# One strided tensor_reduce for unit (1,2), and the first half's sums restored in 32x32 tiles

## What is computed

```python
# block 1
g = groupnorm(x)                                   # 32 groups of 4 channels
q, k, v = einsum('bchw,oc->bohw', g, w_qkv)        # each cut into 4 units of 32 channels
for i, dil in enumerate((1, 2, 4, 8)):             # unit i: 2 heads of 16 channels
    attn = softmax(q . k over the 3x3 neighbours at distance dil)   # 9 scores per pixel
    outs[i] = sum over the 9 neighbours of attn * v                 # neighbours outside the image are 0
x = x + concat(outs[i] * gate[i])                  # gate: softmax over 4 of pooled g
# block 2
p = W_qkv @ groupnorm(x) + b_qkv                   # q = k = v = p, 4 heads of 32 channels
att = softmax(p p^T * scale)                       # 32 x 32 per head
x = x + W_proj @ (att @ p) + b_proj
```

## Time and profile before

| | us |
|---|---|
| median of 3 runs | 83.01 (82.57 to 83.01) |
| the profiled execution | 83.13 |
| its span in the trace | 81.3 |

### The profile page before, as it was taken

One profiled execution on the slowest core, in us unless ns is written; L12 is line 12 of the kernel. 1 busy time (PEld: TensorE's weight loads), 2 busy tenths in 40 slices (PEclk: granted clock), 3 DMA queues, 4 the chain that ended last, 5 costly groups with the idle time before them and its releaser, 6 DMA issues.

```text
span 81.3 us, 2474 instructions
## 1 busy us (share of the span) xinstructions
PE 71.1 (87%) x1010; PEld 51.4 (63%) x1010; DVE 67.5 (83%) x184; ACT 29.3 (36%) x92; POOL 41.5 (51%) x84
## 2 busy tenths in 40 slices
PE   4999998799995698999969797879999999999950
PEld 4999753466742466776857664567676868575530
DVE  2152999999999989999999699889999888597850
ACT  1762765963384000000030003230994271764200
POOL 7104018912930037999999999699990005100000
PEclk9999999999999999999999999999999999999999
DMA  1980055000000000000000000000000000012253
GB/s 27 315 286 18 0 120 142 7 0 8 0 0 4 0 12 0 0 0 4 8 0 0 0 0 0 8 0 0 0 0 8 0 0 12 0 57 72 73 194 129
DMA packets 2796, 3.06 MB, mean 38 GB/s; under 512 B 352, under 2 KB 2400, under 8 KB 2784
## 3 DMA queue, kind: packets, MB, share of 16 engines
q1 hardware_dynamic: 2496, 2.63, 10.5%
q10 hardware_dynamic: 288, 0.26, 0.9%
HBM read 1.84 MB, written 1.05 MB: 36 GB/s over the span
## 4 chain that ended last, share of the span: by engine, by line
DVE 54%; PE 28%; POOL 7%; issue 5%; ACT 2%; POOLq 0%
PE ps L815 27%; DVE qk L602 18%; DVE pv L643 12%; POOL rstd L342 3%; POOL acc L379 3%; DVE acc L655 3%; DVE pv L655 2%; DVE x L674 2%; DVE prob L622 2%; DVE smax L609 2%; DVE ssum L619 2%; POOL pv L379 2%; DVE sums L570 1%; DVE acc L643 1%; PE ps L972 1%
## 5 line engine op out<-in xcount | busy, mean ns | idle before, releaser
L815 PE MATMUL ps<-prob,sel 64*128 64x192 f32 (+6 forms) x192 | 17.8, 313 | 2.7 <-DVE pv L643 1.6
L643 DVE TENSOR_TENSOR pv<-ps,v 128x128 f32<-128x128 f32 (+7 forms) x32 | 17.1, 567 | 1.8 <-PE ps L815 0.8
L815 PEld LDWEIGHTS ps<-prob,sel 64*128 64x128 f32 x192 | 13.7, 186 | 6.9 <-DVE pv L643 3.5
L815 PE MATMUL ps<-xn,wp 128*32 128x256 f32 (+1 forms) x208 | 17.1, 384 | 0.9 <-ACT q L417 0.7
L815 PE MATMUL ps<-idle 128*128 128x128 f32 x82 | 14.6, 328 | 1.1 <-DVE idle L533 1.1
L379 POOL TENSOR_TENSOR pv<-pv 128x240 f32<-128x240 f32 (+3 forms) x24 | 14.1, 600 | 0.5 <-DVE pv L643 0.5
L815 PEld LDWEIGHTS ps<-idle 128*128 128x128 f32 x82 | 12.6, 231 | 2.4 <-DVE idle L533 1.1
L342 POOL TENSOR_TENSOR rstd<-gvar,mhalf 128x2 f32<-128x2 f32 (+1 forms) x6 | 4.9, 809 | 15.9 <-DVE gvar L549 15.9
L379 POOL TENSOR_TENSOR acc<-acc,pv 128x256 f32<-128x256 f32 (+4 forms) x20 | 12.7, 640 | 0.5
L815 PEld LDWEIGHTS ps<-xn,wp 128*32 128x32 f32 (+1 forms) x208 | 8.7, 116 | 6.1 <-ACT xn L443 1.3
L602 DVE TENSOR_TENSOR qk<-q,k 128x672 f32<-128x672 f32 (+7 forms) x21 | 11.4, 607 | 0.0
(11 more groups left out here) (82 smaller groups left out, 89.6 us busy)
## 6 DMA issues: line engine op xcount, KB each, us to landing
out_dram<-x SPq DMA_DIRECT2D x8, 128.0 KB, 1.8
gx<-x_dram SPq DMA_DIRECT2D x2, 256.0 KB, 4.4
gx<-x_dram ACTq DMA_DIRECT2D x2, 128.0 KB, 3.1
sel<-selc_dram SPq DMA_DIRECT2D x4, 64.0 KB, 2.2
wp<-wpack_dram SPq DMA_DIRECT2D x1, 194.0 KB, 4.2
gx<-x_dram SPq DMA_DIRECT2D x1, 192.0 KB, 2.8
wp<-wpack_dram SPq DMA_DIRECT2D x1, 131.0 KB, 2.2
gx<-x_dram SPq DMA_DIRECT2D x1, 128.0 KB, 3.0
```

What stands on the lines that cost most here:

```text
L643: last = nc.vector.tensor_tensor(o, a, b, ALU.mult)
L815: return nc.tensor.matmul(o, w, m, start=start, stop=stop)
```

## The change

**The sum of unit (1,2).** The eight adds on DVE go. In their place one `tensor_reduce` sums the nine slots of `pv[2]`, 256 outputs of nine inputs each, where neighbouring inputs of one output lie 256 elements (1 KB) apart. So that all nine slots can be read in full, `pv[2]` is zeroed once at the start of the kernel on DVE, and the centre product of unit (1,2) goes to slot 4 of `pv[2]` instead of `acc`. The reduction stands behind all products.

**The sum of unit (1,3).** DVE's two adds (`add_last_column`) go, and PE takes slots 6 and 8 into its sums: 12 tiles of four matmuls instead of 10. `sum_second` now waits in three steps: unit (1,0) and all of (1,3) first, then POOL's unit (1,1), then DVE's unit (1,2).

**The first half.** `restore` now brings back all four images at once, in 16 matmuls of 32x32 tiles instead of two times eight matmuls of 128 rows.

**The orders.** In `RSQRT_AFTER` the power of group 0 moves behind the seventh add of unit (1,0), from behind the fifth. `norm(2,1)` moves from ACT to DVE. In the second half the orders of DVE, ACT and PE are written anew, cut to their core here:

```diff
-RSQRT_AFTER = ((1, 0, 4), (1, 1, 0))
+SUMMED_WHOLE = (2,)
+
+RSQRT_AFTER = ((1, 0, 6), (1, 1, 0))
...
+            for s in SUMMED_WHOLE:
+                nc.vector.memset(pv[s][:], 0.0).then_inc(products_zeroed, 1)
...
-                    if ci == 1 and n == 1:
+                    if ci == 1 and n == 1 and not (ph and s in SUMMED_WHOLE):
                         o = view(acc, (ph * ND + s) * N, [[W, rows], [1, nc_]])
...
             def add_neighbours(ph, s):
...
-                    o, a, b = operands(ph, s, n, target, slot)
-                    nc.vector.tensor_tensor(o, a, b, ALU.add).then_inc(dve_added, 1)
...
+                dve.wait_ge(pv_ready, 12 * ph + 3 * s + 3)
+                nc.vector.tensor_reduce(acc[:, ph, s, :], view(pv[s], 0, [[1, N], [N, KK]]), AX.X,
+                                        ALU.add).then_inc(dve_added, 1)
...
+            def add_tiles(ph, tiles, stop, finished=False):
+
+                for s, slot in tiles:
+                    if slot == 4:
+                        t, first, (r0, r1), (c0, c1) = acc, (ph * ND + s) * N, (0, H), (0, W)
+                    else:
+                        ci, ri = divmod(slot, 3)
+                        t, first, (r0, r1), (c0, c1) = pv[s], slot * N, valid_rows(s, ri), columns(DIL[s], ci)[:2]
                     dims = [[W, r1 - r0], [1, c1 - c0]]
                     at = r0 * W + c0
                     for j in range(SLOTS):
                         rows = slice(32 * j, 32 * j + 32)
...
+                        last = mm(view(ps, 512 * (BANK[GROUPS // PHASES * ph] + j) + at, dims, 32 * s, 32),
+                                  ident[rows, rows], view(t, first + at, dims, 32 * j, 32),
+                                  start=slot == 4, stop=(s, slot) in stop)
+                        if finished and (s, slot) == tiles[-1]:
                             last.then_inc(restored, 1)
...
+            def restore():
+
+                pe.wait_ge(added, ADDS * POOL_SUMS[0])
+                pe.wait_ge(prob_ready, PHASES)
+                pe.wait_ge(qk_ready, ND * PHASES)
+                pe.wait_ge(id_loaded, 16)
+                whole = [(s, 4) for s in range(ND)]
+                add_tiles(0, whole, whole, finished=True)
+
+            def sum_second():
+
+                s = LAST_UNIT
                 pe.wait_ge(pv_ready, 12 * PHASES)
+                pe.wait_ge(added, ADDS * POOL_SUMS[0] + ADDS)
+                add_tiles(1, [(0, 4)] + [(s, slot) for slot in (4, 3, 5, 1, 0, 2, 7, 6, 8)], [(0, 4), (s, 8)])
                 pe.wait_ge(added, ADDS * sum(POOL_SUMS))
...
+                add_tiles(1, [(1, 4)], [(1, 4)])
+                pe.wait_ge(dve_added, 1)
+                add_tiles(1, [(2, 4)], [(2, 4)], finished=True)
```

More of the change, by code:

```diff
@@ L193, in build @@
         cells_set = sem("cells_set")
+        products_zeroed = sem("products_zeroed")
         idle_set = sem("idle_set")
@@ L493, in _ @@
                 norm(0, i)
+            copy_projection(0, 0)
             for i in range(2):
                 norm(1, i)
[L496 to L505, removed]
+            copy_projection(0, 1)
+            copy_pT(0, 0)
             squares(2)
             squares(3)
-            copy_fused(0, 1)
[L509 to L515, removed]
+            copy_pT(0, 1)
+            copy_projection(1, 0)
+            copy_projection(1, 1)
+            attention_exp(0)
+            copy_projection(2, 0)
+            copy_pT(1, 0)
+            copy_projection(2, 1)
+            copy_pT(1, 1)
+            for i in range(2):
+                copy_projection(3, i)
+            attention_exp(1)
+            copy_fused(0, 1)
+            for i in range(2):
+                copy_pT(3, i)
             attention_exp(2)
-            copy_pT(3, 1)
+            for i in range(2):
+                copy_fused(1, i)
             attention_exp(3)
@@ L634, in multiply_pv @@
                     dve.wait_ge(added, ADDS * (s + 1))
+                if c == 0:
+                    dve.wait_ge(products_zeroed, len(SUMMED_WHOLE))
                 c0, c1, co = columns(DIL[s], ci)
@@ L795, in _ @@
                 norm(3, i)
-            copy_pT(2, 0)
-            second_residual(0, 0)
-            copy_pT(2, 1)
-            second_residual(0, 1)
+            attention_divide(0)
+            for i in range(2):
+                copy_pT(2, i)
+            copy_fused(0, 0)
+            attention_shift(1)
+            attention_divide(1)
             attention_shift(2)
+            for i in range(2):
+                second_residual(0, i)
             attention_divide(2)
@@ L1064, in _ @@
             spread(1, 3, 0)
-            for i in range(2):
-                project_second(0, i)
+            project_second(0, 0)
+            spread(1, 3, 1)
+            spread(1, 3, 2)
+            project_second(0, 1)
+            transpose(0, 0)
+            sum_second()
+            transpose(0, 1)
             for i in range(2):
                 project_second(1, i)
+            group_stats(2)
+            group_stats(3)
+            attention(0)
+            transpose(1, 0)
             for i in range(2):
-                transpose(0, i)
@@ L1071, in _ @@
-            for i in range(1, 3):
-                spread(1, 3, i)
-            transpose(1, 0)
-            attention(0)
+                project_second(2, i)
             transpose(1, 1)
+            for i in range(2):
+                project_second(3, i)
+            for i in range(2):
+                transpose(2, i)
             attention(1)
-            sum_second()
             for i in range(2):
                 fuse(0, i)
-            pe.wait_ge(ashift_ready, 2)
-            keep_clock(2, BANK[1] + 1)
@@ L1082, in _ @@
-            group_stats(2)
-            finish(0, 0)
-            keep_clock(2, BANK[1] + 1)
-            group_stats(3)
-            finish(0, 1)
-            keep_clock(1, BANK[1] + 1)
+            for i in range(2):
+                transpose(3, i)
+            attention(2)
+            for i in range(2):
+                finish(0, i)
             for i in range(2):
                 fuse(1, i)
+            attention(3)
             for i in range(2):
-                project_second(2, i)
-            transpose(2, 0)
@@ L1093, in _ @@
-            project_second(3, 0)
-            transpose(2, 1)
-            project_second(3, 1)
-            attention(2)
-            for i in range(2):
-                transpose(3, i)
-            finish(1, 0)
-            attention(3)
-            finish(1, 1)
+                finish(1, i)
             for i in range(2):
```

83 lines of the change are left out of this document (18 added, 65 removed).

## The result

The changed kernel is slower: the ratio to the kernel before is 1.0061, 95% interval 1.0038 to 1.0084. Beside a median of 82.79 us of the kernel before (20 executions), that is 83.3 us, where I had forecast 81.6 with a range of 80.5 to 83.2 and a chance of 0.14 for slower by over 1%. The ratio is made of the 8 of 20 executions that ran at full TensorE clock; in the other 12 the mean granted clock was 0.92 to 0.98 and they took 84.9 to 88.0 us, so that the plain median of all 20 is 84.97.

A forecast was written before the change was run, and what follows sets the result against it. DVE was taken to bound the kernel up to the residuals at 65.08, then PE for 14.0 us. Residuals come 3.4 us earlier, PE gives most back, leaving 1.4 us: 81.6 us, range 80.5 to 83.2.

The forecast's parts named there:

- the price of the reduction: On DVE behind all products: 2304 inputs at a 1 KB step take 2.5 us, ending at 61.4.
- The rival: The reduction pays for its step: at twice the price a loss of 1.1 us, 84.1; decides from 3.9 us; chance 0.13.
- A smaller term: Between reduction and residuals of phase 1: four matmuls left on PE, 0.3 us with the hand-over.
- The tail: PE part from the residuals of phase 1 at 61.7 to fuse(2,0) at 73.3, then 4.33 us to the end.
- the tail gives all back: Behind the residuals: six hand-overs of groups 0 to 2 each cost 0.2 us more; time 82.8; chance 0.22.
- the tail is worth more: From residuals to fuse(2,0): no PE wait gives 80.4, half the waits 81.0; chance 0.13.
- The first half's lateness counts: Group 0's variance is 1.2 us later; if POOL waits for it, the tail shifts: 82.3; chance 0.07.
- the memset: Kernel start, DVE: zeroing pv[2], 2304 elements, takes 2.0 us and costs 0.
- The cover: Kernel start: DVE's 2.23 us wait for the first DMA, until 3.67, hides the zeroing with some 0.2 us to spare.
- the restore in tiles: First half, PE: 16 matmuls take 0.55 us before DVE's residual at 49.56 and cost nothing.
- the five idle matmuls that left the tail: PE part behind the residuals: their removal takes off 1.4 us with their waits.

The follow-up runs named there:

- the run with eight steps: Changed kernel plus 13 DVE instructions behind its last residual, the first eight being reductions of pv[2] at differing steps; step 256 took 4.02 us, kernel time not given.
- the run with the norms first: Kernel with mixed products, two idle matmuls and transpose(1,1) moved earlier, plus group 3's bias and norms ahead of group 0's softmax shift; ratio 0.9870, median 81.59 us.
- contiguous inputs: Changed kernel with the reduction reading nine neighbouring elements of pv[2], so summing wrong ones; 81.66 us in the one of four executions at clock 0.995.
- gap filled: Changed kernel with six idle matmuls on PE in its 1.6 us wait for the reduction; five of six executions took 85.1 to 87.9 us.
- mixed products: Changed kernel with unit (1,2)'s products written so that each pixel's nine are neighbours and the reduction reads contiguously; ratio 0.9900 to the kernel before.

## Why the prediction was wrong

**Direction and size.** I forecast 1.4 us faster and got 0.5 slower, at full clock. The forecast and the result differ by some 1.9 us (the last residual ends at 79.61, where I had 77.65), and the prediction's own steps place them.

**The step that failed: the price of the reduction.** "I take 2.5, since the price of the strided row (748) lies on the line of contiguous ones." It measured 4.12. The row that I leant on is a reduction out of PSUM; the run with eight steps shows no price for a step in PSUM (0.42 us for 252 inputs at a step of 28 and of 1), and 1.6 times the time in SBUF (4.02 against 2.6). The term was mis-sized by 1.55 us from start to start, and that is nearly all of the error. The rival had the mechanism, a bound (5.0), and the point from which it decides (3.9 us), which is also what came: at 4.12 the kernel was a little slower than before. It had 0.13. The Trainium skill's rule, set down beside that rival, pointed at exactly this instruction, no row spoke against it for a read of SBUF, and a row from another memory was taken as if it did.

**A smaller term.** Between the end of the reduction (62.91) and the first residual (63.60) 0.7 us pass; I had put 0.3. It is the four last matmuls with both hand-overs, and DVE's wait for them is 0.71 in all the profiles that have them behind its sum. The 1.55 and the 0.4 make the 1.9.

**What was right.** The products end at 58.86 (58.9), though with luck: gvar of group 1 ended 0.3 us sooner than I had it (55.16 against 55.45), and DVE then waited 0.28 us, which I had not, ahead of the centre of unit (1,3). gsq and gvar of group 1 wait for POOL: 0.54 and 0.65 us for two elements each, ending with POOL's adds (54.48 and 55.16 against 54.46 and 55.14). A bias of 0.14 us at 55.71 was not held by POOL's power, as I had assumed. POOL's last add ends at 60.6 (I had 61.0). The tail takes 2.0 us more than before: 11.69 us from residuals to fuse(2) against my 11.6 (3.95 up to the projections of group 2, where I had 3.75, and 7.74 behind them, where I had 7.85), with PE waiting 1.26 us in it (I had 1.2) and then closed. The rivals "the tail gives all back" and "the tail is worth more" are both out: its length was as priced, and it is bound first by group 2's chain, then by PE's work, as the run with the norms first shows. "The first half's lateness counts" is out too: POOL waited 0.42 us.

**Half right: the memset.** 1.98 us as priced, and it costs nothing. But DVE stood still for 0.55 us ahead of it and began at 1.69, while POOL was zeroing a tile of its own from 0.84 to 1.79. That POOL held it was not tried, and the kernel before speaks against a simple form of it: there two memsets of 48 elements ran at 1.25 and 1.33, beside the same memset of POOL, in 0.10 us each. The first sum starts at 3.87 instead of 3.67, and the next step is still at 6.37, since it waits for PE's group statistics, which start at 5.90 behind PE's idle matmuls in both kernels. The cover was not the one I named; there was a second one behind it.

**The term that I had not in the sum at all: the clock.** I wrote that the restore in tiles takes PE's work away from between the later products, "that frees PE, which is not late there", and I counted the five idle matmuls that left the tail as a gain. A PE that is freed can lose its clock. Of this kernel's executions 12 of 20 did, and took 1.7 to 4.7 us more than the 83.2 of the others, which at its worst is more than anything that I weighed. Where they lost it no profile of this very kernel shows, since the profiled execution is one at full clock. The profiles of three kernels close to it (contiguous inputs, gap filled, mixed products) have it in the tail, behind 65 us, and the first of them behind the restore too, at 54 us. In the page of the kernel before the granted clock is full in all slices, with the idle matmuls standing beside it.

## What to carry to other kernels

Price an instruction by a row with the same operation and the same memory and step on its inputs; where there is none, a rival with a chance of its own is not enough, and the forecast has to sit between the ends. Eight small instructions that wait for another engine may cost little in themselves: look at what they take when that engine is still, and try them in another place, before they are replaced. Work taken from TensorE in a stretch with waits is not free: count what is left between the waits, and put idle matmuls there before trusting a gain. And one profile at full clock does not clear a kernel of it, as only the clocks of all 20 executions showed here.

## What the runs showed of the hardware

A float32 `tensor_reduce` of 2304 inputs a partition out of SBUF took 2.54 to 2.6 us at steps of one and two elements and 4.0 to 4.3 at steps of four to 256, POOL idle or not. Out of PSUM (252 inputs, 0.42 us at steps of 28 and 1), and in a `tensor_scalar` of 2304 elements at a step of 256 (2.60 us), a step had no such price. A `tensor_tensor` that writes SBUF at a step of nine elements paid about 0.65 ns an element more (1.32 us against 0.89 for 640 elements). A memset of 2304 elements on DVE started 0.55 us late while POOL was in a memset, two of 48 elements did not; the cause was not tried.

The granted TensorE clock fell to 0.50 after waits of PE of 1.07 and 1.25 us with 1.1 us of work between them; its mean was 0.93 to 0.96 in all four executions of that kernel. In part of the executions of others it fell after waits of 0.50 and 0.41 us with 0.4 us of work between them, and after waits of 0.30, 0.44 and 0.52 us. It held in all 40 executions of the five kernels in which idle matmuls, or in one place a transpose, stood in these waits. It held, too, in the kernel before, which has waits of 0.72 and 0.42 us at 50.4 to 53.6 with 2.1 us of work between them, so a single wait of that length does not decide it. Where the border lies stays open.
